# Two attention stages of a four-layer kernel: GpSimd adds the expert rows of the last group, VectorE takes the other groups at other places

## The chip, the core and the metric

The kernel runs on one core of a Trainium2 chip. Its engines are TensorE (PE in the profile, its weight loads PEld), VectorE (DVE), ScalarE (ACT), GpSimd (POOL) and SyncE (SP, which issues most DMAs). The metric is the device time of one execution in microseconds (us), as the median of several runs.

## The reference, cut to what matters

`x` is 32 tiles of 128 rows by 128 columns, float32. Four layers follow one another, and each adds an attention and a mixture of experts:

```
x = x + attention_l(layernorm(x), ctx)          # l = 0 .. 3
x = x + experts_l(layernorm(x))                 # top-2 of 8 experts in layers 0 to 2, top-1 in layer 3
...
mixed = sum over k of topk_weight[k] * expert_output[chosen[k]]
```

In layer 1 experts have a capacity. What an expert layer adds is, for each row, its k = 0 and k = 1 expert row, each times one weight of that row. The kernel does this sum at the start of the next attention.

## The kernel before, in words

**Groups, streams and turns.** The 32 tiles are 8 groups of `G` = 4 tiles. The second attention (`attention_1`, layer 1) and the fourth (`attention_3`, layer 3) run `W` = 4 groups side by side, one per stream w = 0 to 3, in `TURNS` = 2 turns: turn 0 has groups 0 to 3, turn 1 groups 4 to 7. Each engine has one instruction stream, which it executes in order, and waits on semaphores for the others. `weave` writes the streams' steps in turns: first step of each stream, second step of each, and so on.

**What DVE does in a turn.** `head_norms` normalises the four groups. Then come the steps of `body`. In `attention_1` they are: the query minus its maximum (`less_max`, L1673 and L1674, after PE's `q`); the quotient (L1686 to L1693, after PE's `out`); and the add of the projection with the statistics of the tail (L1696 and `stats_of`, after PE's `proj`). In `attention_3` they are the score maximum (L2484, after `scores`), the reciprocal of the sums (L2488, after ACT's `exp`) and the add of the mixed rows (L2493, after `mixed`). `tail_norms` normalises again, PE turns the rows and multiplies them with the router, and `tail_dve` (L557 to L571) picks experts.

**The next rows.** Before a turn can be normalised, its x rows must have got the expert rows of the layer before. `combine` does that for a group: 8 `scalar_tensor_tensor` (L523), 4 for k = 0 and 4 for k = 1, each `x = row * weight + x` on 128x128, all operands in SBUF. `known` then takes the mean and variance of the group's rows (`bn_stats` L460, `bn_aggr` L456). `next_rows(dve, ch, i, st, here, rounds)` is a generator: at each round it does `here` and `known` for as many groups as `rounds` says, and yields. For turn 0 all four groups come at the start. For turn 1 it is woven behind the bodies of turn 0 with rounds (2, 2): groups of streams 0 and 1 after the first step of the bodies, those of 2 and 3 after the second step.

**Where the rows come from.** `load_pairs` on SP issues 8 loads of 512 KB (L1562), one per group, each with the k = 0 and k = 1 rows; that of turn 1 is issued when the same stream's load of turn 0 has landed. `pairs_here[w]` counts landings.

**GpSimd.** It has no instruction in `attention_1`. In `attention_3` it only issues the scatters at the end of a turn (L2408).

Of the kernel before, what the change touches and what calls it, by code (L numbers as in the profile page):

```python
# [4 lines left out]


# [1 line left out]

# [85 lines left out]
def weave(bodies):  # L94


    bodies = list(bodies)
    while bodies:
        bodies = [b for b in bodies if next(b, "end") != "end"]
# [14 lines left out]
def build(nc, A, out):  # L114
    with ExitStack() as top:
# [11 lines left out]
        def counter(name):  # L127
            return Counter(top.enter_context(nc.semaphore(name)))
# [112 lines left out]
        turned_kept = counter("turned_kept")  # L241
        scales_made = counter("scales_made")
        tail_ready = counter("tail_ready")
        tail_stored = counter("tail_stored")
        tail_turned_made = counter("tail_turned_made")
        tail_kept = counter("tail_kept")
# [240 lines left out]
        def next_rows(dve, ch, i, st, here, rounds):  # L487

            if i < TURNS:
                w = 0  # L490
                for n in rounds:
                    for _ in range(n):
                        here(i, w)
                        known(dve, ch, st, w, x_tile(i * W + w))
                        w += 1
                    yield
                assert w == W

        def combine_stream(dve, ch, i, w, layer):

            if layer in SCATTERED:
                dve.wait_ge(pairs_here[w].sem, i * 16 + (pairs_here[w].value + 16))
            else:
                dve.wait_ge(rows_here.sem, i * W + (w + rows_here.value + 1))
            combine(dve, ch, i * W + w, layer)

        def close_streams(SS, ctx=False):
            for c in (spread_known, roots_made):
# [6 lines left out]
        def combine(dve, ch, g, layer):  # L515

            slots = CHOICES[layer]
            for k in range(slots):
                for j in range(G):
                    t = g * G + j  # L520
                    xt = flat(X[:, bass.ds(t, 1), :])
                    row = YY[:, bass.ds(t, 1), k, :] if layer in SCATTERED and slots == 2 else (XN, Y1)[k][:, bass.ds(t, 1), :]
                    ins = dve.scalar_tensor_tensor(xt, flat(row), WT[:, k, bass.ds(t, 1)], xt, ALU.mult, ALU.add)  # L523
                ch.link(ins)
# [11 lines left out]
        def norm_tiles(ph):  # L536
            return {"stats": sb_in(ph, "norm_stats", [P, W * G, 6]), "mv": sb_in(ph, "mean_var", [P, W * G, 2]),
                    "rstd": sb_in(ph, "rstd", [P, W * G]), "logs": sb_in(ph, "spread_logs", [P, W * G]), "work": sb_in(ph, "newton", [P, 3, W * G])}
# [1092 lines left out]
        def attention_1(layer_before):  # L1631
            assert layer_before in SCATTERED
            with ExitStack() as ph:
# [4 lines left out]
                for w in range(W):  # L1638
# [5 lines left out]
                    t["tl"] = tail_tiles(ph, t["u"], t["uT"], w)  # L1644
                    T.append(t)
                st, st_tail = norm_tiles(ph), norm_tiles(ph)
                block = ph.enter_context(nc.Block())

                @block.sync
                def _(sp):  # L1650
# [9 lines left out]
                @block.vector  # L1660
                def _(dve):
                    ch = Chain(dve)

                    def heads(ap):
                        return ap.rearrange("p (h c) -> p h c", c=8)

                    def wide(ap):
                        return ap.unsqueeze(2).to_broadcast([P, G * 16, 8])

                    def less_max(t, name, rows):  # L1670

                        red = t["red"][:, 0, :].rearrange("p (j h) -> p j h", h=16)
                        ch.link(dve.tensor_reduce(red, rows, AX.X, ALU.max))  # L1673
                        return dve.tensor_tensor(t[name].rearrange("p (j h c) -> p j h c", h=16, c=8), rows, red.unsqueeze(3).to_broadcast([P, G, 16, 8]), ALU.subtract)  # L1674

                    def here(i, w):
                        combine_stream(dve, ch, i, w, layer_before)

                    def body(w, i, S, t):
                        g, A_, B_ = i * W + w, t["A"], t["B"]  # L1680
                        dve.wait_ge(S.pe.sem, S.PE.at(i, "q"))
                        less_max(t, "q", A_.rearrange("p (j h c) -> p j h c", h=16, c=8)).then_inc(S.dve.sem, S.DVE.tick("q_less"))
                        yield
                        dve.wait_ge(S.pe.sem, S.PE.at(i, "out"))
                        three = A_[:, 0:3 * KX].rearrange("p (j c) -> p j c", c=KX)
                        dve.reciprocal(t["dinv"][:, 0:3, :], three[:, :, P:KX])  # L1686
                        ch.link(dve.reciprocal(t["dinv"][:, 3, :], B_[:, P:KX]))
                        o, q = flat(t["u"][:, :, :]), t["q"].rearrange("p (j h c) -> p j h c", h=16, c=8)
                        dve.tensor_tensor(t["u"][:, 0:3, :].rearrange("p j (h c) -> p j h c", c=8), three[:, :, 0:P].rearrange("p j (h c) -> p j h c", c=8),
                                          t["dinv"][:, 0:3, 0:16].unsqueeze(3).to_broadcast([P, 3, 16, 8]), ALU.mult)  # L1690
                        dve.tensor_tensor(heads(t["u"][:, 3, :]), heads(B_[:, 0:P]), t["dinv"][:, 3, 0:16].unsqueeze(2).to_broadcast([P, 16, 8]), ALU.mult)
                        ch.link(dve.tensor_tensor(q, q, t["dinv"][:, :, 16:32].unsqueeze(3).to_broadcast([P, G, 16, 8]), ALU.mult))
                        dve.tensor_tensor(o, o, t["q"], ALU.add).then_inc(S.dve.sem, S.DVE.tick("o"))  # L1693
                        yield
                        dve.wait_ge(S.pe.sem, S.PE.at(i, "proj"))
                        ch.link(dve.tensor_tensor(flat(group(X, g)), flat(group(X, g)), A_[:, :], ALU.add))  # L1696
                        stats_of(dve, st_tail, w, x_tile(g))
                        yield
                    for _ in next_rows(dve, ch, 0, st, here, (W,)):
                        pass  # L1700
                    ch.link()
                    for i in range(TURNS):
                        head_norms(dve, ch, i, SS, st, T)
                        weave([body(w, i, SS[w], T[w]) for w in range(W)] + [next_rows(dve, ch, i + 1, st, here, (2, 2))])
                        ch.link()
                        tail_norms(dve, ch, i, SS, st_tail, T, taken=True)
                        weave(tail_dve(dve, ch, i * W + w, i, SS[w], T[w]["tl"], T[w]["A"]) for w in range(W))

                @block.scalar
# [63 lines left out]
                        weave(body(w, i, SS[w], T[w]) for w in range(W))  # L1773
                close_streams(SS)
                close_rows(layer_before)


        KVT = SETB[:, 0:B * 2 * P].rearrange("p (b k) -> p b k", k=2 * P)
# [586 lines left out]
        def attention_3(layer_before):  # L2365
            SCALE = float(P) ** -0.5
            with ExitStack() as ph:
# [13 lines left out]
                place = sb_in(ph, "place3", [P, N, E])  # L2381
                ends, region = sb_in(ph, "ends3", [P, E]), sb_in(ph, "region3", [P, E])
                spot_f = sb_in(ph, "spot3", [P, N])
                spots = flat(IX[:, :, :])[:, 168:168 + TURNS * N].bitcast(U32).rearrange("p (i t) -> p i t", i=TURNS)
                scratch = carve(flat(Y1[:, :, :]), 2048, [P, 8, TILES_TOP2])
                marks = carve(flat(Y1[:, :, :]), 2048 + 8 * TILES_TOP2, [P, TILES_TOP2, E])
# [13 lines left out]

                @block.gpsimd
                def _(pool):
                    for i in range(TURNS):
                        for w in range(W):
                            pool.wait_ge(SS[w].act.sem, SS[w].ACT.at(i, "tail_kept"))
                            pool.wait_ge(positions_made.sem, NG + i * W + w + 1)
                            for t in range(w * G, (w + 1) * G):
                                pool.indirect_dma_start(xb, bass.IndirectOffsetOnAxis(ap=spots[:, i, t:t + 1], axis=0), ROWS[:, i * N + t, :], None).then_inc(rows_spread.sem, 16)  # L2408
# [69 lines left out]
                def _(dve):  # L2478
# [26 lines left out]
                        dve.tensor_copy(spots[:, i, own], spot_f[:, own]).then_inc(positions_made.sem, 1)  # L2505

                    def here(i, w):
                        combine_stream(dve, ch, i, w, layer_before)
                    for _ in next_rows(dve, ch, 0, st, here, (W,)):
                        pass  # L2510
                    for i in range(TURNS):
                        head_norms(dve, ch, i, SS, st, T)
                        weave([body(w, i, SS[w], T[w]) for w in range(W)] + [next_rows(dve, ch, i + 1, st, here, (2, 2))])
                        ch.link()
                        tail_norms(dve, ch, i, SS, st_tail, T)
                        for w in range(W):
                            weave([tail_dve(dve, ch, i * W + w, i, SS[w], T[w]["tl"], T[w]["A"], [hot])])
                            if w:
                                placed(i, w - 1)
                        placed(i, W - 1)  # L2520
# [6 lines left out]
                    dve.reciprocal(WT[:, 0, :], scratch[:, 7, 0:B])  # L2527
                close_streams(SS)
                close_rows(layer_before)

        experts(0)
        attention_1(0)
# [28 lines left out]
```

## Time and profile before

| | |
|---|---|
| median of 3 runs | 1773.26 us (1766.41 to 1776.73) |
| profiled execution, its own time (the span) | 1780.2 us |
| busy: PE, DVE, ACT, POOL | 1444.8, 1162.8, 818.9, 764.0 us |
| `attention_1`, first load to last DVE instruction | 378.8 to 529.3 us |
| `attention_3`, first load to last scatter | 1518.7 to 1663.9 us |

The profile is of one execution. Its timeline gives for a run of instructions the start, the time from first start to last end, the engine, the line, the operation, the tiles, the count, and in brackets how long the engine sat idle before it and what ended that. Instructions of one engine overlap a little, so that starts, not ends, are what is subtracted. "PEclk" is the clock granted to TensorE in tenths of 2.4 GHz; the other level is 1.2 GHz, half of it.

### The profile page before, as it was taken

Reading aid. Unit: us, or ns where it says so; the run is one execution under the profiler, and the core shown is the slowest. Engines: PE = TensorE matmul, PEld = TensorE weight load, DVE = VectorE, ACT = ScalarE, POOL = GpSimd, SP = SyncE. Lnnn points to the kernel's source line nnn. Section 1 sums busy time; section 2 is a strip of 40 time slices with the busy share of each in tenths; the row PEclk is TensorE's granted clock in tenths of the full one; section 3 lists DMA queues with packets and bytes.
Section 4 is the critical chain, followed back from the end, with each engine's and each line's share of the span. In section 5 each row is a group of like instructions: output and inputs, shape, how many; then the busy total and the mean of one; then the engine's idle time right before and its main releaser. Section 6 shows DMA issues by size and latency. Waiting matters only on the chain. (4 is left out here: it accounts for less than half of the span.)

```text
span 1780.2 us, 37318 instructions
## 1 busy us (share of the span) xinstructions
PE 1444.8 (81%) x10610; PEld 1313.5 (74%) x10611; DVE 1162.8 (65%) x3689; ACT 818.9 (46%) x2528; POOL 764.0 (43%) x757
## 2 busy tenths in 40 slices
PE   6686699927767489999999999999997698446494
PEld 4565499925556389999999999999996698235494
DVE  5657744448675467778787777878785565585343
ACT  4252255512212166666666666666663233314252
POOL 3137344410003454546556565647463466012442
PEclk9696899966667699999999999999998799767697
DMA  9101122230121300000000000000000232500224
GB/s 236 21 19 58 48 59 62 62 111 1 48 94 49 118 13 1 13 1 18 9 17 7 15 9 13 10 0 12 1 13 13 76 84 76 189 12 15 73 64 120
DMA packets 94154, 82.79 MB, mean 47 GB/s; under 512 B 17076, under 2 KB 81047, under 8 KB 93927
## 3 DMA queue, kind: packets, MB, share of 16 engines
q1 hardware_dynamic: 74952, 52.24, 10.6%
q0 software_dynamic: 11936, 24.55, 4.2%
q10 hardware_dynamic: 7168, 4.86, 1.0%
q8 instruction: 42, 0.69, 0.2%
q14 instruction: 56, 0.46, 0.1%
HBM read 51.93 MB, written 31.25 MB: 47 GB/s over the span
## 5 line engine op out<-in xcount | busy, mean ns | idle before, releaser
L1980 POOL TENSOR_TENSOR paired_rows<-paired_rows,rinv 128x1024 f32<-128x1024 f32 x128 | 242.3, 1893 | 288.3 <-DVE rinv L2263 284.8
L2254 DVE TENSOR_TENSOR probs_turned_lo<-psum_banks,probs_turned_hi 128x512 fp32r<-128x512 f32 x256 | 175.6, 686 | 99.7 <-ACT probs_turned_hi L2128 92.9
L2146 ACT ACTIVATE paired_rows<-psum_banks,neg_max 128x256 f32<-128x256 f32 x512 | 237.4, 490 | 0.2
L2027 PE MATMUL psum_banks<-y_turned_parts,queries_hi 128*128 128x256 f32 x1024 | 201.4, 294 | 3.0 <-DVEq L1881 3.0
L2062 PE MATMUL psum_banks<-probs_turned_hi,y_rows 128*128 128x512 f32 x512 | 191.8, 415 | 0.4 <-issue 0.4
L2128 ACT CAST probs_turned_hi<-psum_banks 128x512 fp32r<-128x512 f32 x256 | 151.1, 590 | 56.8 <-PE psum_banks L2011 54.3
L2268 DVE TENSOR_REDUCE neg_max<-psum_banks 128x4 f32<-128x1024 f32 x128 | 156.4, 1222 | 8.9 <-PE psum_banks L2027 4.7
L2027 PEld LDWEIGHTS psum_banks<-y_turned_parts,queries_hi 128*128 128x128 f32 x1024 | 159.2, 192 | 3.6 <-issue 3.6
L2011 PE MATMUL psum_banks<-ident,paired_rows 128*128 128x128 f32 x1024 | 154.7, 274 | 7.7 <-DVEq L1881 4.4
L2128 ACT CAST queries_hi<-psum_banks 128x512 fp32r<-128x512 f32 x128 | 75.0, 586 | 174.7 <-PE psum_banks L2050 168.3
L2027 PE MATMUL psum_banks<-y_turned_parts,queries_lo 128*128 128x256 f32 x512 | 145.3, 284 | 0.0
L2074 PEld LDWEIGHTS psum_banks<-expert_w_a,paired_rows 128*128 128x128 f32 x1024 | 133.8, 191 | 11.9 <-DVE paired_rows L2278 0.7
L2050 PE MATMUL psum_banks<-expert_w_b,expert_w_a 128*128 (+1 forms) x1024 | 139.0, 279 | 2.8 <-ACT tail_turned L2118 1.8
L2074 PE MATMUL psum_banks<-expert_w_a,paired_rows 128*128 128x128 f32 x1024 | 134.8, 274 | 0.5 <-issue 0.5
L2050 PEld LDWEIGHTS psum_banks<-expert_w_b,expert_w_a 128*128 128x128 f32 x1024 | 126.5, 194 | 6.3 <-ACT tail_turned L2118 3.2
L2011 PEld LDWEIGHTS psum_banks<-ident,paired_rows 128*128 128x128 f32 x1024 | 119.8, 142 | 10.3 <-DVEq L1881 5.1
L2254 DVE TENSOR_TENSOR queries_lo<-psum_banks,queries_hi 128x512 fp32r<-128x512 f32 x128 | 88.5, 692 | 42.3 <-ACT queries_hi L2128 35.8
L1410 POOL DMA_INDIRECT expert_rows<-expert_rows_sb,tile_rows x71 | 70.6, 994 | 103.1 <-DVE expert_rows_sb L1497 103.1
L1470 ACT ACTIVATE hidden<-psum_banks,tile_w 128x128 f32<-128x128 f32 x284 | 81.2, 368 | 71.0 <-PE psum_banks L1436 71.0
L2146 ACT ACTIVATION_READ_ACCUMULATOR paired_rows<-psum_banks,neg_max 128x1 f32 x512 | 113.4, 221 | 0.0
L2062 PEld LDWEIGHTS psum_banks<-probs_turned_hi,y_rows 128*128 128x128 f32 x512 | 96.4, 188 | 17.1 <-issue 0.5
L2062 PE MATMUL psum_banks<-probs_turned_lo,y_rows 128*128 128x512 f32 x256 | 100.8, 394 | 0.0
(691 smaller groups left out, 3330.1 us busy)
## 6 DMA issues: line engine op xcount, KB each, us to landing
paired_rows<-expert_rows SPq DMA_DIRECT2D x16, 512.0 KB, 6.0
tile_rows<-rows_by_expert SPq DMA_DIRECT2D x110, 64.5 KB
tile_rows<-rows_by_expert_first SPq DMA_DIRECT2D x71, 64.5 KB
expert_w_b<-in_L_ffn_w_dram SPq DMA_DIRECT2D x2, 2048.0 KB, 12.7
tile_rows<-expert_rows SPq DMA_DIRECT2D x8, 512.0 KB, 3.6
x_rows<-in_x_dram SPq DMA_DIRECT2D x8, 256.0 KB, 5.3
normed_rows_dram<-paired_rows SPq DMA_DIRECT2D x1, 2048.0 KB, 8.7
expert_w_a<-in_L_ffn_gate_up_w_dram SPq DMA_DIRECT2D x1, 2048.0 KB, 9.5
```

Of the source, the lines that this page charges most:

```text
L1410: pool.indirect_dma_start(ys, bass.IndirectOffsetOnAxis(ap=to, axis=0), yo[:, i % SLOTS, :], None).then_inc(expert_out[i % SLOTS].sem, 16)
L1470: ins = act.activation(hidT[:, s % 2, c * P:(c + 1) * P], hidden_bank(s, c // 2)[:, c % 2 * P:(c % 2 + 1) * P], ACT.Gelu, bias=w1[:, s % 4 ...
L1980: ins = pool.tensor_tensor(probs[:, p, :, :], probs[:, p, :, :], rinv[:, p, :].unsqueeze(2).to_broadcast([P, 4, 256]), ALU.mult)
L2011: ins = pe.transpose(bank[T_BANK][:, h * P:(h + 1) * P], probs[:, par, h, c * P:(c + 1) * P], ident[:, :])
L2027: ins = pe.matmul(bank[S_BANKS[par] + h // 2][:, (h % 2) * 256:(h % 2 + 1) * 256], queries[q][:, h, :], yparts[:, 2 * s2 + y, :], start=(k ...
L2050: ins = pe.matmul(bank[Q_BANK][:, h * P:(h + 1) * P], wqk[:, 4 * u3 + h, :], flat(KVT[:, bass.ds(b3, 1), P:2 * P]), start=True, stop=True)
L2062: ins = pe.matmul(bank[Z_BANK][:, :], yrows[:, 2 * s1 + y, k * P:(k + 1) * P], probsT[p][:, (u + 1) % 2, k, :], start=(k == 0 and n == 0), ...
L2074: ins = pe.matmul(bank[Y_BANK][:, 0:P], mixed[:, par, h, :], wvo[:, 4 * u0 + h, :], start=(u0 == 0 and h == 0), stop=(u0 == 3 and h == 3), ...
L2128: ins = act.copy(dst, bank[bank_][:, :])
L2146: ins = act.activation(probs[:, par, h, :], bank[S_BANKS[par] + h // 2][:, (h % 2) * 256:(h % 2 + 1) * 256], ACT.Exp, bias=nmax[:, par, h: ...
L2254: ins = dve.tensor_tensor(lo, bank[bank_][:, :], hi.bitcast(F32), ALU.subtract)
L2268: ins = dve.tensor_reduce(nmax[:, par, :], ps[:, S_BANKS[par]:S_BANKS[par] + 2, :].rearrange("p r (h k) -> p (r h) k", k=256), AX.X, ALU.m ...
```

## The change

GpSimd gets a new function that does the combination of the last group of turn 1 (tiles 28 to 31) with whole-group operations, as a product and a sum for each k. DVE no longer does L523 for that group; it waits for a new semaphore and takes only the statistics. The rounds of the next rows change: in `attention_1` from (2, 2) to (1, 1, 1, 0, 1), where the first is run right after `head_norms`, the next three are woven and the last comes after `tail_norms`; in `attention_3` from (2, 2) to (2, 1, 0, 1), the first right after `head_norms`, the rest woven. Each stage gets one new tile `weighted` (128x4x128 float32).

```diff
+        def add_late_group(pool, weighted, layer):
+            g, w = NG - 1, W - 1
+            own = slice(g * G, (g + 1) * G)
+            pool.wait_ge(pairs_here[w].sem, pairs_here[w].value + 16 * TURNS)
+            for k in range(2):
+                pool.tensor_tensor(weighted[:, :, :], YY[:, own, k, :], WT[:, k, own].unsqueeze(2).to_broadcast([P, G, P]), ALU.mult)
+                pool.drain()
+                ins = pool.tensor_tensor(X[:, own, :], X[:, own, :], weighted[:, :, :], ALU.add)
+                if k == 0:
+                    pool.drain()
+            ins.then_inc(late_group_added.sem, 1)
...
# attention_1
+                @block.gpsimd
+                def _(pool):
+                    add_late_group(pool, weighted, layer_before)
...
                     def here(i, w):
-                        combine_stream(dve, ch, i, w, layer_before)
+                        if i and w == W - 1:
+                            dve.wait_ge(late_group_added.sem, late_group_added.value + 1)
+                        else:
+                            combine_stream(dve, ch, i, w, layer_before)
...
                         head_norms(dve, ch, i, SS, st, T)
-                        weave([body(w, i, SS[w], T[w]) for w in range(W)] + [next_rows(dve, ch, i + 1, st, here, (2, 2))])
+                        ahead = next_rows(dve, ch, i + 1, st, here, (1, 1, 1, 0, 1))
+                        next(ahead, None)
+                        weave([body(w, i, SS[w], T[w]) for w in range(W)] + [itertools.islice(ahead, 3)])
                         ch.link()
                         tail_norms(dve, ch, i, SS, st_tail, T, taken=True)
+                        for _ in ahead:
+                            pass
...
# attention_3: the same here(), add_late_group ahead of the scatters, and
-                        weave([body(w, i, SS[w], T[w]) for w in range(W)] + [next_rows(dve, ch, i + 1, st, here, (2, 2))])
+                        ahead = next_rows(dve, ch, i + 1, st, here, (2, 1, 0, 1))
+                        next(ahead, None)
+                        weave([body(w, i, SS[w], T[w]) for w in range(W)] + [ahead])
```

## Rows read from the trace of the kernel before

**Rows 1.** The page: span, and TensorE's granted clock in 40 equal slices.

```profile
span 1780.2 us, 37318 instructions
...
PEclk9696899966667699999999999999998799767697
```

**Rows 2.** Timeline of DVE in `attention_1`, turn 0.

```profile
394.89 2.32 DVE L523 SCALAR_TENSOR_TENSOR x_rows<-paired_rows,mix_weights,x_rows 128x128 f32<-128x128 f32 x8
...
408.19 0.69 DVE L1673 TENSOR_REDUCE head_sums<-psum_banks 128x64 f32<-128x512 f32 x1 [3.75 <-PE psum_banks L1743]
...
417.19 2.35 DVE L523 SCALAR_TENSOR_TENSOR x_rows<-paired_rows,mix_weights,x_rows 128x128 f32<-128x128 f32 x8
...
424.48 0.73 DVE L1686 RECIPROCAL d_inv<-psum_banks 128x96 f32<-128x96 f32 x1
...
436.76 2.35 DVE L523 SCALAR_TENSOR_TENSOR x_rows<-paired_rows,mix_weights,x_rows 128x128 f32<-128x128 f32 x8
...
444.06 0.65 DVE L1696 TENSOR_TENSOR x_rows<-x_rows,psum_banks 128x512 f32<-128x512 f32 x1
...
450.33 1.17 DVE L456 BATCH_NORM_AGGREGATE mean_var___<-norm_stats___ 128x2 f32<-128x6 f32 x16
...
459.71 0.19 DVE L557 COPY tail_logits____<-psum_banks 128x32 f32<-128x32 f32 x1 [2.44 <-PE psum_banks L588]
```

**Rows 3.** Timeline of DVE in `attention_1`, turn 1.

```profile
488.01 0.76 DVE L1686 RECIPROCAL d_inv<-psum_banks 128x96 f32<-128x96 f32 x1 [2.58 <-PE psum_banks L1762]
...
504.14 0.69 DVE L1696 TENSOR_TENSOR x_rows<-x_rows,psum_banks 128x512 f32<-128x512 f32 x1 [3.75 <-PE psum_banks L1743]
```

**Rows 4.** Timeline of PE in `attention_1`, turn 0.

```profile
436.90 1.12 PE L620 MATMUL psum_banks<-ident,u_rows___ 128*128 128x128 f32 x4 [1.96 <-DVE u_rows___ L1693]
...
445.66 1.16 PE L1743 MATMUL psum_banks<-wsmall,u_turned___ 128*128 128x128 f32 x8
```

**Rows 5.** Timeline of DVE in `attention_3`, start and turn 0.

```profile
1533.49 2.32 DVE L523 SCALAR_TENSOR_TENSOR x_rows<-paired_rows,mix_weights,x_rows 128x128 f32<-128x128 f32 x8
...
1550.62 0.69 DVE L2484 TENSOR_REDUCE neg_max<-psum_banks 128x4 f32<-128x512 f32 x1 [7.65 <-PE psum_banks L2427]
...
1554.15 2.35 DVE L523 SCALAR_TENSOR_TENSOR x_rows<-paired_rows,mix_weights,x_rows 128x128 f32<-128x128 f32 x8
...
1569.72 1.09 DVE L2493 SCALAR_TENSOR_TENSOR x_rows<-psum_banks,rinv,x_rows 128x128 f32<-128x128 f32 x4
...
1573.98 3.40 DVE L460 BATCH_NORM_STATS2 norm_stats_____<-x_rows 128x6 f32<-128x128 f32 x16
```

**Rows 6.** Timeline of PE in `attention_3`, turn 0.

```profile
1557.90 5.38 PE L2435 MATMUL psum_banks<-ctx_rows,expert_w_a 128*128 x32
```

**Rows 7.** Groups of POOL by shape: busy time, mean ns of one, idle before.

```profile
L1925 POOL TENSOR_TENSOR paired_rows<-tile_rows,group_scale 128x512 f32<-128x512 f32 x14 | 14.6, 1040 | 2.0
L1927 POOL TENSOR_TENSOR x_rows<-x_rows,paired_rows 128x512 f32 x10 | 12.8, 1284 | 1.9 <-issue 1.9
```

**Rows 8.** The page's DMA issues: count, size, median us to landing.

```profile
paired_rows<-expert_rows SPq DMA_DIRECT2D x16, 512.0 KB, 6.0
```

**Rows 9.** The SP loads of `paired_rows`, whole run: ns, first and last start.

```profile
L1562 SPq DMA_DIRECT2D paired_rows<-expert_rows x16: 359/378/1495, 378.8 to 1527.0; - x16
```

**Rows 10.** The same in 388 to 389 us, the last load of `attention_1`.

```profile
L1562 SPq DMA_DIRECT2D paired_rows<-expert_rows x1: 360/360/360, 388.5 to 388.5; - x1
```

**Rows 11.** Timeline in the third attention, POOL and DVE beside each other.

```profile
955.22 0.41 POOL L1908 COPY y_turned_copy<-expert_w_b 128x256 f32 x1
955.39 0.26 DVE L431 TENSOR_TENSOR rows_work<-rows_work 128x8 f32<-128x8 f32 x1
...
1048.48 0.17 DVE L431 TENSOR_TENSOR rows_work<-rows_work 128x8 f32<-128x8 f32 x1
...
1049.03 0.73 POOL L1910 TENSOR_TENSOR y_turned_parts<-expert_w_b,y_turned_parts 128x256 fp32r<-128x256 f32 x1 [1.12 <-issue]
1049.06 0.79 DVE L2180 COPY scale_of_rows<-rows_rstd 128x4 f32 x2 [0.16 <-issue]
```

More of the change, by code:

```diff
@@ L7 @@
 from contextlib import ExitStack
+import itertools
 import concourse.bass as bass
@@ L243, in build @@
         tail_ready = counter("tail_ready")
+        late_group_added = counter("late_group_added")
         tail_stored = counter("tail_stored")
@@ L1646, in attention_1 @@
                 st, st_tail = norm_tiles(ph), norm_tiles(ph)
+                weighted = sb_in(ph, "weighted1", [P, G, P])
                 block = ph.enter_context(nc.Block())
+                @block.gpsimd
+                def _(pool):
+                    add_late_group(pool, weighted, layer_before)
                 @block.sync
@@ L1775, in attention_1 @@
                 close_rows(layer_before)
+                late_group_added.value += 1
         KVT = SETB[:, 0:B * 2 * P].rearrange("p (b k) -> p b k", k=2 * P)
@@ L2383, in attention_3 @@
                 spot_f = sb_in(ph, "spot3", [P, N])
+                weighted = sb_in(ph, "weighted3", [P, G, P])
                 spots = flat(IX[:, :, :])[:, 168:168 + TURNS * N].bitcast(U32).rearrange("p (i t) -> p i t", i=TURNS)
@@ L2402, in _ @@
                 def _(pool):
+                    add_late_group(pool, weighted, layer_before)
                     for i in range(TURNS):
@@ L2507, in here @@
                     def here(i, w):
-                        combine_stream(dve, ch, i, w, layer_before)
+                        if i and w == W - 1:
+                            dve.wait_ge(late_group_added.sem, late_group_added.value + 1)
+                        else:
+                            combine_stream(dve, ch, i, w, layer_before)
                     for _ in next_rows(dve, ch, 0, st, here, (W,)):
@@ L2529, in attention_3 @@
                 close_rows(layer_before)
+                late_group_added.value += 1
         experts(0)
```

## The prediction, made before the changed kernel ran

> **What bounds the kernel now.** I read the page first: span 1780.2 us, and a granted TensorE clock that stands near 9 tenths in most slices of 44.5 us (1780.2 / 40) but at 6 or 7 in slices 8 to 13, where `attention_1` lies [rows 1]. So these stages are not TensorE at its rate; who sets their pace must be read from a timeline. DVE's timeline in turn 0 of `attention_1` is the view that decides: from the start of the next rows at 417.19 to the aggregates at 450.33 no row has an idle time in brackets [rows 2]. DVE works without a pause for 33 us, and what it does includes four groups of next rows. PE stands behind it: its last turn of the quotient starts when DVE has delivered it [rows 4]. Turn 1 has no next rows, so it shows how long DVE would wait for PE if nothing filled the gap: 2.58 us before the quotients, 3.75 us before the projection adds [rows 3]. In `attention_3` the picture is the same, and starker: PE has finished its last mixed product at 1557.90 + 5.38 = 1563.28 [rows 6], and DVE comes to it only from 1569.72 on [rows 5]. In both, a microsecond of DVE in turn 0 is a microsecond of the kernel.
>
> **One group's price.** Two groups of next rows take 424.48 - 417.19 = 7.29 us, so one takes 3.64, of which the eight additions are 2.35 and the statistics 1.3 [rows 2].
>
> **`attention_1`, before the adds.** The group of stream 0 moves to just behind `head_norms`, where DVE waits 3.75 us for PE's `q` [rows 2]; 3.64 fits, so it costs nothing, with 0.1 us to spare. If that wait were shorter (PE at its full clock), the excess would show. The group of stream 1 stays between `less_max` and the quotients. It covers the wait of 2.58 us that would be there anyway [rows 3]. The quotients thus start 3.65 us earlier, at 420.83, and keep their 436.76 - 424.48 = 12.28 us [rows 2], to 433.1. The group of stream 2 goes behind them, into the wait of 3.75 us that turn 1 shows [rows 3]: nothing again.
>
> **`attention_1`, the adds.** Now PE is late next. From the start of its last turn (436.90) to the end of the last projection (445.66 + 1.16 = 446.82) it takes 9.92 us [rows 4]; that start moves 3.65 us ahead, to 433.25, so the last projection ends at 443.17. DVE adds one group and takes its statistics in (450.33 - 444.06) / 4 = 1.57 us [rows 2], done at 444.8. The aggregates start 5.5 us earlier than 450.33. The last group's statistics (1.3 us) come behind `tail_norms`, where DVE waits 2.44 us for the logits [rows 2]: hidden. **Gain 5.5 us.**
>
> **`attention_3`.** Streams 0 and 1 (7.29 us) go into the wait of 7.65 us before the score maxima [rows 5]: nothing, with 0.36 us to spare. The maxima end at 1554.15; stream 2's group brings DVE to 1557.8, when PE is just starting the mixed products [rows 6]; the four small reciprocals are then covered by PE too. The last product ends at 1563.28, its addition takes (1573.98 - 1569.72) / 4 = 1.07 us [rows 5], and then, inside the weave, come the 1.3 us of statistics of the last group. The tail's statistics start at 1563.28 + 0.05 + 1.07 + 1.3 = 1565.7 instead of 1573.98 [rows 5]. **Gain 8.2 us.** Together 13.7 us; turn 1 and the stages behind start from the end of these chains (loads of weights are issued by the same chain or long before), so I pass it on whole.
>
> **What GpSimd costs.** A product of 128x512 takes 1.04 us and a sum 1.28 us [rows 7]; two of each are 4.64 us. GpSimd's result is needed only after `tail_norms` in `attention_1` and at about 1564 in `attention_3`; it starts some 50 and 30 us before. The DVE wait on it is therefore free. But where does it start? When the eighth load lands: 388.5 + 6.0 = 394.5, and 1527.0 + 6.0 = 1533.0 [rows 8 to 10]. At 394.89 and 1533.49 DVE starts the eight additions of stream 3 for turn 0 [rows 2, 5], and these lie at the head of the stage, where PE and ACT have nothing to do: no cover at all.
>
> **The two engines beside each other.** In the third attention, a DVE operation on two SBUF tensors that started inside a GpSimd copy took 0.26 us where it takes 0.17 otherwise, and ended at 955.65, 0.02 us after the copy. Two small DVE copies that started inside a GpSimd operation took 0.79 us and ended at 1049.85, GpSimd's at 1049.76 [rows 11]. So DVE stands still until about 0.15 us before the recorded end of GpSimd's. L523 reads two SBUF tensors. Each of GpSimd's four operations would hold back one addition; between two, in GpSimd's drain, one slips through, and eight are enough to meet all four. Price: 4.64 less 4 x 0.15 is 4.04; of the first about 0.5 us is over when the additions come. 3.5 us in each stage. The bounds are 0 (the additions get through) and 4.64 in each. I take 3.5, since the rows show the standstill for this kind of operand, if only for tiny ones. **Loss 7.0 us.**
>
> The Trainium skill says it as a rule that speaks against this change ("SBUF — State Buffer", section "Who interferes with whom"): a DVE instruction with two SBUF inputs contends with a GpSimd instruction that reads SBUF, and the one that issues first keeps the shared ports for its whole instruction. The trace's rows agree but for the last 0.15 us; by the rule to the letter the loss would be about 4.1 us a stage and the sum 5.5 us.
>
> **Sum.** 5.5 + 8.2 - 7.0 = 6.7 us. Against the profiled execution's own time of 1780.2 that is 1773.5. The median of the runs is 6.9 us below it; there the forecast is 1773.26 - 6.7 = **1766.6 us**, 0.38% less. About 0.5% (8.9 us) is what a measurement of this kernel can tell from no change.
>
> **Rivals.** (a) *The additions get through.* If a stream of DVE additions does not stand still as single tiny ones do, nearly nothing is lost and 12.5 to 13.7 us remain: 1759.6 to 1760.8. Against it are [rows 11]; for it, that no row shows eight in a row beside GpSimd.
> (b) *DVE holds the port while it has additions queued.* GpSimd then gets in only at the drain between k = 0 and k = 1 and behind the additions. DVE loses 0.5 at first, one sum (1.28 - 0.15 = 1.1), and then something at its scale and normalise operations from the two that are left (1.04 and 1.28), some 0.8: 2.4 us a stage. Gain 13.7 - 4.8 = 8.9, 1764.4, right at the bound.
> (c) *The cover is too short.* The three fits of 0.1, 0.1 and 0.36 us hang on TensorE's clock, and the adds in `attention_1` follow PE at whatever clock it is granted there. At twice the clock the wait of 3.75 us before `less_max` would be no shorter than 1.9, and the first group would stick out by up to 1.7. If PE's 9.92 us before the last add grew by a fifth, another 2 would go. Together 2 to 4 us less: 1768.6 to 1770.6.
> (d) *The other side: the granted clock behind the stages.* The clock fell and rose at places that follow PE's pauses, and these all shift. If one slice of the long stretch that stands at 9 tenths [rows 1] stood at 6, PE work of 44.5 us would take up to 44.5 x (0.9 / 0.6 - 1) = 22 us more. The change is slower by over 0.5% from a loss of 6.7 + 8.9 = 15.6 us on, so that about 0.7 of a slice decides; a full one gives 1766.6 + 22 = 1788. For it speaks only that slices at 6 and 9 alternate early in the kernel.
>
> **How the numbers follow.** Forecast with its own range 1763.5 to 1768.5: 0.45. (a) 0.20, (b) 0.14, (c) 0.15, (d) 0.06. The range from 1759 to 1772 takes in the bound of no loss at its low end (1759.6), and at its high end (c) and the bound of 4.64 us a stage (1768.9) with the 3 us that the median of three may be off; outside lie (d) and strays. Faster by over 0.5% is below 1764.4: all of (a), half of (b), and a fifth of the forecast's own spread: 0.20 + 0.07 + 0.09 = 0.36. Slower is (d), with a little for strays: 0.07. The rest, 0.57, is within 0.5%.
>
> **What the profile after would show.** In `attention_1`: L523 of stream 3, turn 0, taking not 2.32 but about 5.8 us beside four GpSimd operations (rival (a): about 2.4); no idle time over 0.2 us before L1673; the quotients right behind 3.64 us of next rows; then an idle time of up to 1 us between the adds, with PE named; statistics of the last group before L557 with no wait on GpSimd. In `attention_3`: L2493 starting within a microsecond or two of PE's first mixed product, the maxima after at most 0.5 us idle. The prediction is wrong if GpSimd's operations lie elsewhere than beside stream 3's additions, if PE's steps in turn 0 get slower than in these rows, or if the third attention or the expert stages change their length by more than 3 us.

## The result, and the profile after

| | before | after |
|---|---|---|
| median, 20 runs of each | 1781.49 us (1766.41 to 1788.85) | 1772.62 us (1763.10 to 1778.28) |
| ratio | | 0.9948, 95% interval 0.9933 to 0.9963 |
| span of the profiled execution | 1780.2 us | 1770.9 us |

By the ratio the kernel is 0.52% faster, 9.3 us of 1781.49 (the medians differ by 8.9), where 6.7 us were forecast. "Faster by over 0.5%" had a chance of 0.36, and the interval reaches to both sides of 0.5%. The forecast as a ratio, 0.9962, lies inside the interval. As a time, 1772.62 lies 0.6 us above the range that ended at 1772.0. The page after, beside [rows 1]:

```profile
span 1770.9 us, 37312 instructions
...
PEclk9686899976658799999999999999998799667697
```

The head of the second attention, DVE and POOL on one timeline (start, length of the run of instructions, engine, line):

```profile
395.96 1.03 POOL L515 TENSOR_TENSOR weighted<-paired_rows,mix_weights 128x512 f32<-128x512 f32 x1 [23.63 <-DMA paired_rows<-expert_rows]
396.50 0.38 DVE L458 BATCH_NORM_AGGREGATE mean_var__<-norm_stats__ 128x2 f32<-128x6 f32 x4
396.79 4.98 DVE L538 SCALAR_TENSOR_TENSOR x_rows<-paired_rows,mix_weights,x_rows 128x128 f32<-128x128 f32 x8
397.15 1.38 POOL L517 TENSOR_TENSOR x_rows<-x_rows,weighted 128x512 f32<-128x512 f32 x1 [0.15 <-issue]
398.68 1.16 POOL L515 TENSOR_TENSOR weighted<-paired_rows,mix_weights 128x512 f32<-128x512 f32 x1 [0.15 <-issue]
399.97 1.39 POOL L517 TENSOR_TENSOR x_rows<-x_rows,weighted 128x512 f32<-128x512 f32 x1
```

The eight additions of stream 3 took 2.32 us before [rows 2] and take 4.98 beside GpSimd: the forecast's standstill, at 2.66 us. Narrower windows show single additions, of which one alone takes about 0.34:

```profile
398.60 0.34 DVE L538 SCALAR_TENSOR_TENSOR x_rows<-paired_rows,mix_weights,x_rows 128x128 f32<-128x128 f32 x1
...
399.01 0.97 DVE L538 SCALAR_TENSOR_TENSOR x_rows<-paired_rows,mix_weights,x_rows 128x128 f32<-128x128 f32 x1
...
399.90 0.34 DVE L538 SCALAR_TENSOR_TENSOR x_rows<-paired_rows,mix_weights,x_rows 128x128 f32<-128x128 f32 x1
```

The second of them waited out the product of 398.68, and two more additions waited out the two sums (1.345 us each, the longest of the run). Between two of GpSimd's operations one addition starts and keeps its own length, and the next one stands: held and free additions take turns, as forecast. The free one ends while GpSimd's next operation already counts as running. GpSimd waits too: its sums take 1.38 us instead of 1.28 [rows 7], its second product 1.16 instead of 1.04.

Turn 0 of the second attention behind that, DVE:

```profile
412.94 0.66 DVE L1693 TENSOR_REDUCE head_sums<-psum_banks 128x64 f32<-128x512 f32 x1
...
421.74 2.35 DVE L538 SCALAR_TENSOR_TENSOR x_rows<-paired_rows,mix_weights,x_rows 128x128 f32<-128x128 f32 x8
...
425.40 0.73 DVE L1709 RECIPROCAL d_inv<-psum_banks 128x96 f32<-128x96 f32 x1
...
437.68 2.35 DVE L538 SCALAR_TENSOR_TENSOR x_rows<-paired_rows,mix_weights,x_rows 128x128 f32<-128x128 f32 x8
...
441.51 0.69 DVE L1719 TENSOR_TENSOR x_rows<-x_rows,psum_banks 128x512 f32<-128x512 f32 x1
...
444.05 0.69 DVE L1719 TENSOR_TENSOR x_rows<-x_rows,psum_banks 128x512 f32<-128x512 f32 x1 [0.91 <-PE psum_banks L1770]
...
449.83 1.26 DVE L458 BATCH_NORM_AGGREGATE mean_var___<-norm_stats___ 128x2 f32<-128x6 f32 x16
...
456.77 0.87 DVE L462 BATCH_NORM_STATS2 norm_stats__<-x_rows 128x6 f32<-128x128 f32 x4
...
460.07 0.19 DVE L572 COPY tail_logits____<-psum_banks 128x32 f32<-128x32 f32 x1 [1.98 <-PE psum_banks L603]
```

Beside [rows 2]: the 3.75 us wait before L1693 is gone, one group (3.66 us) instead of two stands before the quotients, one behind them, and then the second and third adds wait 0.91 us for PE each. The last group's statistics lie in the wait for the logits, which is still 1.98 us. The fourth attention, beside [rows 5]:

```profile
1525.51 5.39 DVE L538 SCALAR_TENSOR_TENSOR x_rows<-paired_rows,mix_weights,x_rows 128x128 f32<-128x128 f32 x8
...
1545.46 0.69 DVE L2514 TENSOR_REDUCE neg_max<-psum_banks 128x4 f32<-128x512 f32 x1
...
1548.99 2.35 DVE L538 SCALAR_TENSOR_TENSOR x_rows<-paired_rows,mix_weights,x_rows 128x128 f32<-128x128 f32 x8
...
1554.92 1.13 DVE L2523 SCALAR_TENSOR_TENSOR x_rows<-psum_banks,rinv,x_rows 128x128 f32<-128x128 f32 x4 [1.36 <-PE psum_banks L2465]
...
1560.79 3.19 DVE L462 BATCH_NORM_STATS2 norm_stats_____<-x_rows 128x6 f32<-128x128 f32 x16
```

The additions take 5.39 us (3.07 more), the maxima start with no idle time in brackets, and the mixed rows now wait for PE.

To compare kernels, each attention is cut at DVE's instructions: the **head** is from the first addition to the first operation of the scales (L436 before, L438 after), **turn 0** from there to the scales of the tail, the **rest** to the next stage (second attention) or to the first logits of turn 1 (fourth). The view of stretches has their length, the busy time of PE, PEld, DVE, ACT and POOL with their instructions in brackets, then PEclk, the DMA share and GB/s. Head, turn 0 and rest of the second attention, before and after:

```profile
383.95:398.74 14.79, 0.00 (x0) 0.00 (x0) 13.77 (x64) 0.00 (x0) 0.00 (x0) 0.50 0.64 201
398.74:451.58 52.84, 34.67 (x152) 26.75 (x152) 42.81 (x153) 9.56 (x18) 0.00 (x0) 0.63 0.00 1
451.58:529.71 78.13, 55.01 (x280) 44.69 (x280) 51.36 (x258) 19.25 (x38) 0.05 (x1) 0.63 0.20 68
```

```profile
385.84:403.30 17.46, 0.00 (x0) 0.00 (x0) 16.43 (x65) 0.00 (x0) 4.95 (x4) 0.50 0.50 157
403.30:451.17 47.87, 34.22 (x152) 26.62 (x152) 39.71 (x137) 9.57 (x18) 0.00 (x0) 0.64 0.00 1
451.17:526.46 75.29, 52.62 (x280) 43.01 (x280) 52.86 (x264) 19.25 (x38) 0.05 (x1) 0.64 0.22 70
```

Head 2.67 us longer, turn 0 4.97 shorter, at nearly the same clock (0.63 and 0.64).

### The profile page after: what moved, and what is told of

Read it like the earlier page. It is cut to its first block and busy times, and to the rows that moved or that the text cites. A ratio compares the mean times of both kernels' runs of the same rounds, so it can differ in the third digit from the quotient of the medians.

```text
span 1770.9 us, 37312 instructions
## 1 busy us (share of the span) xinstructions
PE 1438.6 (81%) x10610; PEld 1308.5 (74%) x10611; DVE 1166.2 (66%) x3673; ACT 819.0 (46%) x2528; POOL 773.6 (44%) x765
## 5 line engine op out<-in xcount | busy, mean ns | idle before, releaser
L2282 DVE TENSOR_TENSOR queries_lo<-psum_banks,queries_hi 128x512 fp32r<-128x512 f32 x128 | 88.5, 692 | 41.3 <-ACT queries_hi L2156 35.7
```

The source lines that it names most:

```text
L2282: ins = dve.tensor_tensor(lo, bank[bank_][:, :], hi.bitcast(F32), ALU.subtract)
```

## Experiments

All profiles, cut in that way (us; "between" is from the end of the second attention to the first addition of the fourth; the columns before it are the second attention, those behind it the fourth):

| profile | head | turn 0 | rest | between | head | turn 0 | rest |
|---|---|---|---|---|---|---|---|
| before | 14.8 | 52.8 | 78.1 | 992.8 | 14.7 | 41.4 | 58.0 |
| before_again | 14.8 | 52.8 | 78.0 | 989.3 | 14.7 | 41.5 | 58.0 |
| after | 17.5 | 47.9 | 75.3 | 988.1 | 17.8 | 33.1 | 61.4 |
| after_again | 17.8 | 43.4 | 77.3 | 990.2 | 17.9 | 32.3 | 57.5 |
| after_third | 17.7 | 45.5 | 75.6 | 990.3 | 17.9 | 32.3 | 57.5 |
| a1_only | 17.7 | 43.4 | 77.3 | 988.0 | 14.7 | 40.8 | 58.1 |
| a3_only | 14.8 | 52.8 | 78.2 | 992.6 | 17.8 | 32.1 | 58.1 |
| rounds_only | 14.8 | 47.8 | 79.9 | 996.5 | 14.7 | 35.7 | 60.4 |
| pool_only | 17.8 | 46.2 | 79.5 | 995.6 | 17.8 | 39.4 | 57.5 |
| late_pool | 14.8 | 46.4 | 75.8 | 991.1 | 14.7 | 33.4 | 57.6 |
| late_again | 14.8 | 46.5 | 79.8 | 987.6 | 14.7 | 33.7 | 61.4 |
| late_plus | 14.8 | 47.8 | 75.3 | 990.9 | 14.7 | 32.1 | 60.4 |
| memset_beside | 14.8 | 46.5 | 79.8 | 988.7 | 14.7 | 32.9 | 57.6 |

| kernel | ratio to before, 95% interval | forecast ratio |
|---|---|---|
| after_again, after_third | 0.9951 (0.9931 to 0.9971), 0.9941 (0.9920 to 0.9962) | 0.9957, 0.995 |
| a1_only | 0.9948 (0.9927 to 0.9970) | 0.9984 or 0.997 |
| a3_only | 0.9965 (0.9940 to 0.9990) | 0.9971 or 0.9986 |
| rounds_only | 0.9974 (0.9953 to 0.9994) | 0.993 |
| pool_only | 1.0023 (1.0002 to 1.0043) | 1.0006 or 0.9974 |
| late_pool, late_again | 0.9933 (0.9912 to 0.9955), 0.9916 (0.9887 to 0.9945) | 0.9915, 0.9917 |
| late_plus | 0.9912 (0.9889 to 0.9936) | 1.3 us below late_pool |

**The two kernels again.** No edit.

> The changed kernel once more, for a ratio on one chip with the three below and for a second profile. Theory 'stretch' (what DVE saves in turn 0 of the two stages is passed on whole): from the first addition to the tail's scale of turn 0, 65.3 us in the second attention (67.6 before) and 50.9 in the fourth (56.2 before), and 7.6 us in all, a ratio of 0.9957. Rival 'clock' (TensorE's granted clock decides what is left of it elsewhere): the same stretches, but the whole differs from 7.6 us by several us either way, and the two profiles of the same kernel differ by as much behind turn 0.

> The changed kernel on the same chip as the two below, and a third profile. Theory 'pace': where DVE no longer sets the pace TensorE does, so turn 0 of the second attention (head scales to tail scales) takes 43.4 us if the granted clock is full from about 24 us after the first addition, and 46 to 48 if only from 34 (both seen), while the head (17.5 to 17.8 us in both stages) repeats. Ratio 0.995 again. Rival: turn 0 repeats within 0.5 us and the rest moves.

> The kernel before once more, for a second profile. Theory 'clock': the stretches from first addition to tail scale stay within 1 us where DVE sets the pace without a pause (67.6 and 56.2 us), while the waits in turn 1 and the time between the two attentions (992.8 us) move by several us with the granted clock. Rival: all of it repeats within 1 us.

The kernel before repeats in its stages: turn 0 of the second attention takes 52.8 us twice and a third time in a3_only, whose second attention is that of before, and its rests repeat to about 0.1 us as well. (Turn 0 of the fourth took 41.4, 41.5 and, in a1_only, 40.8.) Only "between" moved, by 3.6 us. So before_again bears out "clock" for the time between the stages and not for the waits in turn 1. With the new rounds the same code takes 47.9, 43.4 and 45.5 us in turn 0. There neither theory of after_again was right: both had the stretch from the first addition to the tail's scale at 65.3 us, and it was 61.2. The stretches of after_again, head and turn 0 of the second attention, and turn 0 of after_third:

```profile
385.10:402.86 17.76, 0.00 (x0) 0.00 (x0) 16.73 (x65) 0.00 (x0) 4.95 (x4) 0.50 0.56 176
402.86:446.30 43.44, 28.33 (x152) 21.54 (x152) 39.33 (x137) 9.56 (x18) 0.00 (x0) 0.77 0.00 1
```

```profile
400.58:446.08 45.50, 30.84 (x152) 23.20 (x152) 39.51 (x136) 9.57 (x18) 0.00 (x0) 0.69 0.00 1
```

The same 152 matmuls are busy 28.33 us at a granted clock of 0.77, 30.84 at 0.69 and 34.22 at 0.64. The full clock began 24 us after the first addition in after_again and 37 us after it in the first profile; in before it began 34 us after it. In all of them PE had stood still through the head at half clock. What starts it earlier in one execution than in another, these runs do not show. Theory "pace" missed: in after_third the full clock began after 24 us too, and turn 0 took 45.5 us, not 43.4. In after_again the clock, down to half from 42 us on, was full again from 55 to 62 us after the first addition, where the adds lie, and one add waited for PE (0.86 us); in after_third it stayed at half there, and three adds waited 0.91 each. "Between", where the two kernels have the same code, runs from 988.1 to 992.8 in these five profiles: the time outside the two stages moves by 4.7 us, against the 6.7 that the whole change was forecast to give.

DVE does not fill turn 0 of before, though. Between 408 and 416 us it waits four times for PE's `q`, 6.63 us in all, the first time in [rows 2] and then here, at half clock:

```profile
410.73 0.69 DVE L1673 TENSOR_REDUCE head_sums_<-psum_banks 128x64 f32<-128x512 f32 x1 [1.08 <-PE psum_banks L1743]
...
413.27 0.69 DVE L1673 TENSOR_REDUCE head_sums__<-psum_banks 128x64 f32<-128x512 f32 x1 [0.72 <-PE psum_banks L1743]
...
415.81 0.69 DVE L1673 TENSOR_REDUCE head_sums___<-psum_banks 128x64 f32<-128x512 f32 x1 [1.08 <-PE psum_banks L1743]
```

In the three profiles with this code the full clock began 34 us after the first addition each time, behind these waits, which so come out alike, and 52.8 us repeats. In `pool_only`, below, it was full from 24 us on:

```profile
408.75 0.69 DVE L1693 TENSOR_REDUCE head_sums<-psum_banks 128x64 f32<-128x512 f32 x1 [2.62 <-PE psum_banks L1766]
...
413.26 0.68 DVE L1693 TENSOR_REDUCE head_sums___<-psum_banks 128x64 f32<-128x512 f32 x1
```

The first row has the only one of the four waits for PE that is left there, and its turn 0 takes 46.2 us. Of the 6.7 us less, 2.35 are the additions that GpSimd took over and 4.0 are these waits.

**One part at a time.** `rounds_only` leaves GpSimd out and lets DVE add all groups at the new places. `pool_only` keeps rounds (2, 2). `a1_only` and `a3_only` have the whole change in one stage. (In `rounds_only` GpSimd's calls and the tiles `weighted` are gone as well.)

```diff
# rounds_only, both stages
-                        if i and w == W - 1:
-                            dve.wait_ge(late_group_added.sem, late_group_added.value + 1)
-                        else:
-                            combine_stream(dve, ch, i, w, layer_before)
+                        combine_stream(dve, ch, i, w, layer_before)
```

> Only the new rounds; DVE adds all groups itself, and GpSimd does nothing there. If GpSimd's operations hold back DVE's additions at the head (theory 'port'), the eight additions of stream 3 in turn 0 are back at 2.3 us; the stretch in the second attention is 2.7 us shorter than with the whole change, 62.7, and in the fourth 3.1 shorter and 2.35 longer (the last group's additions are DVE's again), 50.2. In the second attention the last group takes 3.64 us in a wait of 3.2 for the logits, so 0.4 us come back there. In all 3 us below the whole change: 0.993. Rival: without GpSimd's help the last group's additions cost more than the port did, and the kernel is slower than the whole change.

> Only GpSimd's additions; the rounds are (2, 2) as before. Theory 'port': eight additions fewer (2.35 us) and 2.7 and 3.1 us lost at the head, so stretches of 68.0 and 56.9 us, and a ratio of 1.0006: the help alone is worth nothing. Rival: the help is worth its 2.35 us in each stage, ratio 0.9974, and the stretches 65.3 and 53.8.

> The change in the second attention alone. Theory 'stretch': the forecast for this stage with the loss as measured at the head, 5.5 - 2.7 = 2.8 us, and nothing elsewhere: ratio 0.9984. Rival 'clock': the second attention lies where TensorE's granted clock changes often, the same kernel had turn-0 stretches of 65.3 and 61.2 us in two profiles, and the stage gives 4 to 6 us: ratio 0.997.

> The change in the fourth attention alone. Theory 'stretch': 8.2 - 3.1 = 5.1 us, ratio 0.9971, and the two stages add up to the whole change (0.9950). Rival 'given back': in the first profile of the whole change 3.4 of 5.2 us were gone again at the end of turn 1, so 2 to 3 us are left: ratio 0.9986.

The heads fall in two classes without exception: 14.7 to 14.8 us where GpSimd is idle beside them, 17.5 to 17.9 where it adds. That is the loss, 2.7 to 3.1 us a stage. The rounds give turn 0 of the fourth attention 5.7 us alone (41.4 to 35.7) and GpSimd's help 2.0 alone (39.4); with both it is 8.3 to 9.3. So there the help is worth about its 2.35 us in turn 0 and costs 3.1 in the head: `pool_only` is not faster, as theory "port" said, and by its ratio slower, if by little. Its stretches were 63.9 and 57.3 us, where "port" had 68.0 and 56.9: the first is shorter by the clock, and the whole time did not get it. In the second attention `rounds_only` has the turn 0 of the first profile of the whole change (47.8 and 47.9, both at clock 0.64): there the last group lies in the wait for the logits, GpSimd's help gives turn 0 nothing, and the head pays 2.7 us for it. A kernel with the new rounds and GpSimd in the fourth attention alone was not run.

The whole times are less tidy. `rounds_only` missed its forecast: its stretches are what theory "port" said (62.6 and 50.4 us for head and turn 0, against 62.7 and 50.2), but its ratio is 0.9974, not 0.993: by whole times it is slower than the whole change, as the rival said, though the stretches do not show the rival's cause. In its one profile "between" is the longest of all (996.5 us) and the rests (79.9 and 60.4) are 1.8 and 2.4 us above those of before; rests as long stand in late_again, late_plus and the first profile of the whole change. `a1_only` gave 0.52%, more than both forecasts, nearer to "clock" (turn 0 43.4 us). `a3_only` gave 0.35%, more than both of its forecasts too, and its rest of 58.1 us gives nothing back, against the rival. 0.52% and 0.35% together are more than the whole change gave in any of three comparisons. The intervals are 0.4% to 0.5% wide each, so that does not prove much. The mean granted clock goes with it: 0.8820, 0.8810 and 0.8825 over the runs of before, 0.8824, 0.8818 and 0.8822 in `rounds_only`, `pool_only` and `a3_only`, but 0.8858 and 0.8866 in the whole change run again and 0.8863 in `a1_only`. The 20 runs of the changed kernel in the first comparison had 0.8832, between the two groups. Less time in a stage of low clock raises that mean by itself, so this is a trace of the effect, not its size. Why the clock stands higher with one arrangement stays open.

**GpSimd elsewhere.** `late_pool` starts GpSimd when DVE reads PSUM.

```diff
+                    add_late_group(pool, weighted, layer_before, (SS[0].pe.sem, SS[0].PE.at(0, "q")))        # attention_1
+                    add_late_group(pool, weighted, layer_before, (SS[0].pe.sem, SS[0].PE.at(0, "scores")))   # attention_3
...
+            if start:
+                pool.wait_ge(*start)
```

> The whole change, but GpSimd starts its four operations only when TensorE has made stream 0's query product (second attention) or scores (fourth), where DVE reads PSUM. Theory 'port': stream 3's additions take 2.3 us again, DVE's operations on PSUM beside GpSimd are as long as before, stretches 62.7 and 47.8 us, and the kernel 5.8 us below the whole change, ratio 0.9915. Rival: DVE is held back by GpSimd wherever it runs, and the 5.8 us only move; ratio 0.995.

> late_pool once more beside the changed kernel. Theory 'port': heads of 14.8 and 14.7 us, 5.8 us below the changed kernel, 0.9917. Rival 'clock': part of it is given to TensorE's clock, as in the first comparison (0.9933 against 0.9951, 3.2 us).

The same view of late_pool in the second attention, where GpSimd now works:

```profile
411.52 0.69 DVE L1696 TENSOR_TENSOR expert_w_a<-psum_banks,head_sums 128x512 f32<-128x512 f32 x1
411.91 1.26 POOL L519 TENSOR_TENSOR x_rows<-x_rows,weighted 128x512 f32<-128x512 f32 x1 [0.15 <-issue]
...
413.33 1.04 POOL L517 TENSOR_TENSOR weighted<-paired_rows,mix_weights 128x512 f32<-128x512 f32 x1 [0.15 <-issue]
413.67 0.69 DVE L1696 TENSOR_TENSOR expert_w_a<-psum_banks,head_sums_ 128x512 f32<-128x512 f32 x1
```

Here neither engine is held back: L1696 reads one operand from PSUM and keeps its 0.69 us, GpSimd is back at 1.04 and 1.26. The heads are 14.8 and 14.7 again, and turn 0 of the second attention does not pay for it (46.4 against 43.4 to 47.9). In the fourth attention it does. Between the maxima, which read PSUM, stand four tiny scalings on SBUF:

```profile
1543.52 1.26 POOL L519 TENSOR_TENSOR x_rows<-x_rows,weighted 128x512 f32<-128x512 f32 x1 [0.16 <-issue]
...
1544.05 0.75 DVE L2517 TENSOR_SCALAR neg_max_<-neg_max_ 128x4 f32<-128x4 f32 x1
```

The same scaling in before:

```profile
1552.29 0.17 DVE L2485 TENSOR_SCALAR neg_max_<-neg_max_ 128x4 f32<-128x4 f32 x1
```

The four take 0.41, 0.75, 0.51 and 0.74 us, each until 0.03 us after the recorded end of a GpSimd operation, and 0.17 each in before. From the first maximum to the additions behind them DVE needs 5.11 us instead of 3.53, and turn 0 takes 33.4 and 33.7 us, against 32.3 to 33.1. So of the fourth attention's 3.1 us about 1.6 only moved: the rival is out in the second attention and half right in the fourth. That leaves 5.8 - 1.6 = 4.2 us. By the ratios the gain over the changed kernel is 3.2 and 4.5 us (0.0018 and 0.0025 of 1777). The means of the runs differ by 3.3 us (95% interval 0.6 to 6.1) between after_again and late_pool, and by 3.4 (-2.2 to 9.0) between after_third and late_again, where the medians are only 0.7 apart. So the first pair alone tells the gain from nothing.

**A GpSimd that only writes.** `late_pool` with six needless fills of the scratch tile in the head:

```diff
+            for _ in range(6):
+                pool.memset(weighted[:, :, :], 0.0)
+                pool.drain()
```

> As late_pool, but when the last load has landed GpSimd first fills its scratch tile with zeros six times (128x512 each, which it need not; the result is the same). GpSimd then writes SBUF beside stream 3's additions and reads nothing. Theory 'port for reads': the eight additions keep their 2.3 us. Rival 'any GpSimd work': each fill of about 0.45 us holds back an addition, and the eight take 4 us or more.

```profile
392.49 3.76 POOL L515 MEMSET weighted<- 128x512 f32 x6 [22.92 <-DMA paired_rows<-expert_rows]
392.80 0.38 DVE L458 BATCH_NORM_AGGREGATE mean_var__<-norm_stats__ 128x2 f32<-128x6 f32 x4
393.10 2.32 DVE L543 SCALAR_TENSOR_TENSOR x_rows<-paired_rows,mix_weights,x_rows 128x128 f32<-128x128 f32 x8
```

The additions lie wholly beside the fills and take 2.32 us. There is one profile of this, with both heads as without GpSimd (14.8 and 14.7 us). Operations of GpSimd that read SBUF hold these additions back; one that only writes does not. This is what the Trainium skill states ("SBUF — State Buffer", section "Who interferes with whom"): a DVE instruction with two SBUF inputs contends with a GpSimd instruction that reads SBUF, not with one that only writes it. The traces here agree, 4.98 and 5.39 us against 2.32.

**The last 1.3 us.** `late_plus` is `late_pool` with the last statistics of the fourth attention behind `tail_norms`.

```diff
-                        ahead = next_rows(dve, ch, i + 1, st, here, (2, 1, 0, 1))
+                        ahead = next_rows(dve, ch, i + 1, st, here, (2, 1, 0, 0, 1))
...
-                        weave([body(w, i, SS[w], T[w]) for w in range(W)] + [ahead])
+                        weave([body(w, i, SS[w], T[w]) for w in range(W)] + [itertools.islice(ahead, 3)])
...
+                        for _ in ahead:
+                            pass
```

> late_pool, with the last group's statistics in the fourth attention moved behind tail_norms, into the wait for the logits (1.8 to 2.7 us there). Theory: DVE's 1.3 us ahead of the tail's statistics go, the stretch is 46.8 instead of 48.1 us, and the kernel 1.3 us below late_pool. Rival: the move is hidden by TensorE's next steps and nothing can be measured.

Head and turn 0 of the fourth attention are 46.8 us together, as said. The ratio, 0.9912, is the lowest of all and 0.0004 (0.7 us) below late_again's on the same chip, which its interval cannot tell from nothing, nor from 1.3 us.

## Why the prediction was right or wrong

**The step that failed is the baseline of the sum**, "the median of the runs is 6.9 us below it; there the forecast is 1773.26 - 6.7". The three runs shown gave 1773.26; twenty gave 1781.49, and the other three comparisons 1776.71, 1778.34 and 1777.69. So the median did not lie 6.9 us below the profiled span of 1780.2 but 1.3 above it. The span was a sign of it: the kernel's times exceed the spans by 1.8 us (1772.66 for the span of 1770.9), so that execution took about 1782 us, 5 more than the slowest of the three. The forecast of 1773.5 for the span was 2.6 us above the 1770.9 that came; on 1781.49 it would have been 1774.8 in time, 2.2 above the 1772.62 measured. The baseline carried a fault of 8.2 us, and 2.2 us more gain than forecast hid part of it.

**The loss beside GpSimd** was the right mechanism at the right place, forecast 3.5 us a stage, measured 2.7 and 3.1. Held and free additions took turns as said. The sizes were off: a standstill cost 1.0 us in a sum and 0.63 in a product (1.345 and 0.97 less 0.34), where the prediction had 1.13 and 0.89 (1.28 and 1.04 less 0.15). In the second attention GpSimd's first product began 0.8 us ahead of the additions (395.96 against 396.79), more than forecast, and was all but over when the first came, so that one held back almost nothing. Rivals (a), that the additions get through, and (b), that DVE keeps the port, fell.

**The gain in turn 0** was forecast at 5.5 and 8.2 us. It was 5.0 and 8.3 in the first profile, with PE late at the adds as said; 9.4 and 9.1, 7.3 and 9.1 in the next two. The step took PE's pace from the one profile of before. It holds at that clock. But the three further waits for PE's `q` that stand in that profile (2.9 us) were not in the sum, and at full clock they go, and one of the two waits at the adds as well. Rival (c) had seen this dependence, but only as a loss: in after_again the first group does stick out of the shorter wait, and turn 0 is 4.4 us shorter than in the first profile all the same.

**"I pass it on whole"** cannot be read from one profile. In the first one 3.4 of the fourth attention's 5.2 us were gone at the end of turn 1 (rest 61.4 us, PEclk 0.69), in the next two nothing was (57.5 us). Over all runs 9.3, 8.7 and 10.5 us arrived (0.0052, 0.0049 and 0.0059 of the medians of before), where head and turn 0 of both stages gave 7.5, 12.4 and 10.4 us in the three profiles. That the first two spans also differ by 9.3 us is luck: 4.7 of it is "between", which was 3.6 us shorter in before_again with no edit. That also met a sign by which the prediction called itself wrong, a change of over 3 us in the expert stages, and it says nothing here, since the kernel before shows one as large. Rival (d) did not come.

## What to carry to other kernels

When work goes from DVE to GpSimd, look at what DVE does at the moment GpSimd's input arrives: if it reads two SBUF tensors with nothing to cover it, hold GpSimd back with a semaphore until DVE reads PSUM. Then look at the small operations in between: four scalings of 128x4 on SBUF gave back half of what that won in the fourth attention. Waits of one engine on another are the places to put work, and the turn without that work shows how long they are. Take the baseline from as many runs as the difference needs, and check the profiled execution's time against it: the median of three runs here was 3 to 8 us off those of 14 to 34, for a gain of 9.

## What the runs showed of the hardware

Of DVE additions of 128x128 on two SBUF tensors beside GpSimd operations 0.15 us apart, one starts in the gap and runs its 0.34 us into the start of GpSimd's next, and the one behind it stands to 0.15 us after that operation's recorded end: 0.97 us beside a product, 1.345 beside a sum. GpSimd loses about 0.1 us in each such operation (1.38 for 1.28, 1.16 for 1.04). Six fills beside the same additions cost them nothing. A DVE scaling of 128x4 on SBUF stood as well (up to 0.75 us for 0.17), operations that read PSUM did not (0.69).

One stretch took 52.8 us in three profiles, in which the full clock began at the same place, while another took 43.4, 45.5 and 47.9 us in three executions of one kernel, with the granted clock at 0.77, 0.69 and 0.64.
